# A residual added in PSUM by TensorE instead of on VectorE, in a bidirectional state-space block

## What is computed

```
xn  = layernorm(x)                                   # over the features
u_d = silu(conv4(win @ xn) + bias_d)                 # d = 0 forward, d = 1 on reversed time; 256 channels
delta, B, C = projections of u_d                     # softplus on delta
h[t] = exp(delta*A) * h[t-1] + delta*B*u             # 16 states for each channel, a scan over 512 tokens
y_d = sum over states (h * C) + D * u_d
attn = ((y_0 + reversed y_1) * silu(wz @ xn)) @ wout
ffn  = quantize(xn @ hadamard) @ ternary(w_ffn)      # 4 bits for each token
out  = x + attn + ffn                                # x is the residual
```

## Time and profile before

| | us |
|---|---|
| median of three runs | 885.19 (882.79 to 886.70) |
| the profiled execution | 887.24 |
| its span from first to last instruction | 885.2 |

### The profile page before, as it was taken

One profiled execution on the slowest core, in us unless ns is written; L12 is line 12 of the kernel. 1 busy time (PEld: TensorE's weight loads), 2 busy tenths in 40 slices (PEclk: granted clock), 3 DMA queues, 4 the chain that ended last, 5 costly groups with the idle time before them and its releaser, 6 DMA issues. The chain is left out here.

```text
span 885.2 us, 12125 instructions
## 1 busy us (share of the span) xinstructions
PE 757.5 (86%) x3953; PEld 390.4 (44%) x3953; DVE 798.4 (90%) x855; ACT 779.7 (88%) x1436; POOL 729.3 (82%) x355
## 2 busy tenths in 40 slices
PE   8867978799897988989799798979989897997885
PEld 6324445253543535344363445435353443634353
DVE  3849899998999999998999989999999989999996
ACT  2699997999979998999989999899989999898870
POOL 0176979798896988889697888979888896978994
PEclk9978999989999999999999999999999999999797
DMA  6435126070441608143180614506071430706100
GB/s 182 124 73 143 37 79 127 3 179 4 120 94 38 145 4 188 31 109 70 38 181 4 162 21 104 112 32 151 4 178 39 104 76 33 174 3 154 26 25 13
DMA packets 55119, 74.83 MB, mean 85 GB/s; under 512 B 6784, under 2 KB 23568, under 8 KB 55056
## 3 DMA queue, kind: packets, MB, share of 16 engines
q1 hardware_dynamic: 54624, 73.79, 35.7%
q10 hardware_dynamic: 432, 0.26, 0.1%
HBM read 62.49 MB, written 11.53 MB: 84 GB/s over the span
## 5 line engine op out<-in xcount | busy, mean ns | idle before, releaser
L752 POOL TENSOR_TENSOR hst<-hst,c_rep 128x1024 f32<-128x1024 f32 x255 | 598.6, 2372 | 103.0 <-DVE hst L627 90.6
L627 DVE TENSOR_TENSOR_SCAN hst<-da,b_ps 128x512 f32<-128x512 f32 x512 | 581.7, 1199 | 27.1 <-issue 21.0
L433 ACT ACTIVATE da<-rep,neg_a 128x511 f32<-128x511 f32 x504 | 331.5, 709 | 6.0 <-DVE hst L627 5.8
L964 PE MATMUL b_ps<-ident,dbx_t 128*128 128x128 f32 x1536 | 238.6, 296 | 97.0 <-DVE hst L627 72.5
L964 PEld LDWEIGHTS b_ps<-ident,dbx_t 128*128 128x128 f32 x1536 | 181.6, 150 | 225.1 <-DVE hst L627 130.4
L420 ACT ACTIVATE dbx_t<-du_t,b_t 128x256 f32<-128x256 f32 x576 | 248.1, 495 | 2.6 <-PE b_ps L964 1.9
L985 PE MATMUL y<-hst,sum_sel 128*32 128x512 f32 x1024 | 149.3, 658 | 4.3 <-POOL hst L752 4.3
L869 PE MATMUL pb<-xnt,conv_wt 128*128 128x512 f32 x240 | 110.7, 604 | 1.6 <-ACT du_t L403 0.9
L762 POOL TENSOR_TENSOR dbx_t<-du_t,b_t 128x1024 f32<-128x1024 f32 x48 | 91.7, 1910 | 7.6 <-ACT du_t L403 7.6
L943 PE MATMUL b_ps<-t_log,spread_sel 32*128 32x512 f32 x256 | 88.8, 666 | 1.7 <-DVE hst L627 1.0
L616 DVE TENSOR_TENSOR b_ps<-b_ps,b_rep 128x1024 f32<-128x1024 f32 x64 | 77.9, 1218 | 3.6 <-PE b_ps L943 2.3
(11 more groups left out here) (135 smaller groups left out, 602.8 us busy)
## 6 DMA issues: line engine op xcount, KB each, us to landing
rep<-d_scr SPq DMA_DIRECT2D x128, 256.0 KB, 9.1
c_rep<-bc_scr SPq DMA_DIRECT2D x64, 256.0 KB, 4.8
d_scr<-t_pos SPq DMA_DIRECT2D x16, 512.0 KB, 3.0
b_rep<-bc_scr SPq DMA_DIRECT2D x64, 64.0 KB, 2.4
x_ln<-x SPq DMA_DIRECT2D x8, 256.0 KB, 3.3
x_res<-x SPq DMA_DIRECT2D x8, 256.0 KB, 3.0
out<-x_res SPq DMA_DIRECT2D x8, 256.0 KB, 7.5
rep<-x SPq DMA_DIRECT2D x7, 256.0 KB, 4.4
```

The lines of the kernel that those rows point to most:

```text
L433: nc.scalar.activation(da[s % 2][:, j, 1:L], rep[d][h][:, j, 1:L], ACT.Exp, scale=neg_a[:, d, h, j, q:q + 1]).then_inc(decay_done, 1)
L627: nc.vector.tensor_tensor_scan(hst[s % RING][:, j, :], da[s % 2][:, j, :], b_ps[:, j, :], 0.0, ALU.mult, ALU.add).then_inc(scan_done, 1)
L752: nc.gpsimd.tensor_tensor(hst[s % RING][:, two, :], hst[s % RING][:, two, :], c_rep[d][:, q:q + 1, :].broadcast_to([P, 2, L]), ALU.mult).t ...
L964: ins = tr(b_ps[:, j, P * c:P * (c + 1)], dbx_t[(NX * d + q - 1) % 2][:, c, NJ * h + j, :, :].rearrange("p r e -> p (r e)"), ident[:, :])
```

## The change

DVE's addition goes away. PE adds the residual instead: ahead of the other products of a token block stands a product of the identity matrix with `x_res`, which opens the sum in the bank. The bank then holds the finished output, and ACT copies it into `x_res` (`keep_out`). PE now waits for `xres_loaded` before it projects. ACT's copy stands in slot 5 of the units with `d = 1` from the second batch on, and once behind the loop for the last batch.

```diff
+            def keep_out(b):
+                act.wait_ge(out_filled, b + 1)
+                nc.scalar.activation(x_res[:, :, :], pb[:, 1, :].rearrange("p (c o) -> p c o", c=NC), ACT.Copy).then_inc(out_ready, 1)
...
                     if s == 5:
                         if d == 0:
                             z_sigmoid(b)
+                        elif not first(b):
+                            keep_out(b - 1)
                         inputs_t(d, U, 3, 2)
...
             batches(act, body)
             keep_xqt(NB - 1)
+            keep_out(NB - 1)
...
-            def add_residual(b, at):
-                dve.wait_ge(out_filled, b + 1)
-                dve.wait_ge(xres_loaded, DMA * (b + 1))
-                nc.vector.tensor_tensor(x_res[:, :, :], at.rearrange("p (c o) -> p c o", c=NC), x_res[:, :, :], ALU.add).then_inc(out_ready, 1)
...
-                    if s == 5 and d == 1 and not first(b):
-                        add_residual(b - 1, pb[:, 1, :])
...
-            add_residual(NB - 1, pb[:, 1, :])
...
                 pe.wait_ge(free, count)
+                pe.wait_ge(xres_loaded, DMA * (b + 1))
                 for c in cs:
                     at = slice(P * c, P * (c + 1))
-                    mm(pb[:, 1, at], xqt[:, at], wq_t[:, :], start=True, stop=False)
+                    mm(pb[:, 1, at], ident[:, :], x_res[:, c, :], start=True, stop=False)
+                    mm(pb[:, 1, at], xqt[:, at], wq_t[:, :], start=False, stop=False)
...
+            pe.wait_ge(xres_loaded, DMA * NB)
             for c in range(NC):
                 at = slice(P * c, P * (c + 1))
-                mm(pb[:, 1, at], xqt[:, at], wq_t[:, :], start=c == 0, stop=False, skip_group_check=True)
+                mm(pb[:, 1, at], ident[:, :], x_res[:, c, :], start=c == 0, stop=False, skip_group_check=True)
+                mm(pb[:, 1, at], xqt[:, at], wq_t[:, :], start=False, stop=False, skip_group_check=True)
```

## The result

| | us |
|---|---|
| before, median of four runs | 884.53 (882.79 to 886.70) |
| after, median of four runs | 920.65 (916.50 to 922.03) |
| ratio | 1.040 (95%: 1.036 to 1.044) |
| span of the profiled execution, before and after | 885.2 and 918.3 |

What follows compares the result with a forecast made beforehand. DVE (90% busy) led, ACT (88%) close; ACT's in-order list decides. Late `keep_dut` 27.7, clock 3.6, last batch 2.8, end 0.8: 34.9 us on a median of 885.19, so 920 us; range 904 to 932.

Steps and rivals of the forecast that it cites:

- ACT's lead turns into a stall: Slot 5, units with d = 1: ACT stands still before its copy until the projection ends, 7 to 8.5 us, seven times.
- DVE waits for the decays: Before slot 5's second pair of scans DVE idles 4 to 4.6 us for ACT's decays; the pair ends 2.8 us late.
- `keep_dut` is late and nothing behind it absorbs that: In units with d = 1, `keep_dut` starts 4.76 or 4.49 us late and each of six batches lengthens by its delay.
- part of the delay is absorbed: Rival: the convolution chain has slack, so only DVE's 2.8 us stay in each batch; 906 us, chance 0.14.
- The size per batch: Batches b = 1 to 6: 27.7 us for late `keep_dut` plus 3.6 us for the clock, 5.2 us each.
- the chain through ACT's stall: From ACT's wait in slot 5 to `keep_dut`: 4.76 or 4.49 us late in each of six batches, 27.7 us in all.
- The end: Last batch: DVE's second pair 2.8 us late; behind the loop, four more products 0.88 less 0.10 for the copy, 0.8 us.
- The clock's term: PE's clock falls after its wait in slot 5, so ACT waits 0.6 us a batch for `du`, 3.6 us in all.
- The products as such: Four identity products a batch on PE, 0.22 us each, make `out_filled` 0.88 us later.
- The faster rival: The wait before `keep_dut`, up to 3.89 us, hides the copy and DVE's gain shows; 877 us, chance 0.03.
- the 8.7 us that I had allowed as its most: Most that taking the addition off DVE could gain: eight additions, 5.4 us, plus the waits before them, 3.3 us.

Runs made afterwards that it cites:

- f_filler: The changed kernel plus 15 thrown-away 128x128 products on PE while it waits in slot 5 for ACT's inputs of slot 6; 920.53 us, 1.041.
- d_copy: The changed kernel with the copy given back to DVE at its addition's place; PE still adds the residual, ACT has nothing new; 893.35 us, 1.010.
- dcopy_z: d_copy plus five PE products with a matrix of zeros in slot 2 of every unit; 887.97 us, 1.004 against the kernel before.
- p3_slot7: The changed kernel with ACT's copy moved from slot 5 to slot 7, directly ahead of `keep_dut`; 885.30 us, 1.003 against the kernel before.
- before_z: The kernel before plus five PE products with a matrix of zeros in slot 2 of every unit; 885.51 us, 1.000.

## Why the prediction was right

The time (920 against 920.65) and the sign were right, and the mechanism is the one that was forecast. By its steps:

- **ACT's lead turns into a stall: right.** Forecast 8.4 us for unit (1, 1), measured 8.39. The six inner batches show 8.39, 6.89, 8.39, 8.45, 6.89 and 8.39. The last batch showed 5.21, well below the 7 to 8.5 that I had given for all seven (6.89 is just below it); I had not looked up ACT's lead there.
- **DVE waits for the decays: right.** Forecast 4 to 4.6 us, measured 4.49 in unit (1, 1); 27.6 us over seven, so less in some.
- **`keep_dut` is late and nothing behind it absorbs that: right.** This was the step with the largest weight and no direct row. Its wait fell to 7.5 us in all (forecast: below 8), its starts are 109.2 us apart (forecast: 108 to 110). The rival "part of the delay is absorbed" (906 us) falls with this. The moves of the copy confirm it: 900, 894 and 885 us.
- **The size per batch: slightly low.** Forecast 31.3 us over six batches, 5.2 each; measured 5.50. Split by the table above, the chain through ACT's stall, with the low stretch behind it, was forecast at 4.6 + 0.6 a batch and is 4.4; low stretches elsewhere add 1.1, for which the forecast had nothing. The first batch came to 2.7 instead of 5.4; if the head start of 2.1 us is added, it is 4.9. The end was forecast at 3.6 and came to 2.9. The errors offset each other; that the median is met to 0.7 us is partly luck.
- **The clock's term: near in size, wrong in place.** I had 0.6 us a batch for the wait that ACT has for the transposes of `du` at the lower clock. The low stretch came, where forecast, and ACT waited 0.0 to 0.4 us for it; by `f_filler` it costs 0.1 to 0.2 us a batch. The wrong step is the assumption that this is the place where the clock matters, and that elsewhere it stays as it was. The 1.1 us come from the other low stretches; the section on the hardware below has two such places.
- **The end: right.** Twelve groups of products instead of eight; the sum of states and DVE's product behind them:

```profile
907.44 0.46 PE L1110 MATMUL pb<-x_res,ident 128*128 128x128 f32 x2 [3.13 <-DVE y_gated L640]
...
911.92 1.06 PE L986 MATMUL y<-hst,sum_sel 128*32 128x512 f32 x8
...
913.05 0.69 DVE L640 TENSOR_TENSOR y_gated<-y,gate 128x512 f32<-128x512 f32 x1 [5.87 <-PE y L986]
```

  The products took 4.48 us instead of 2.69, 1.8 more and twice the 0.88 that I had added, since the low clock now fell on them; but then the sum of states ran at full clock, 1.06 instead of 1.94. From the first product to DVE's multiplication it is 5.61 against 4.69, 0.92 more.
- **The products as such (0.88 us a batch on the way to `out_filled`): right for the changed kernel.** On their own `d_copy` came out 2 us above the forecast interval for it, but not by the products' work, which costs 0.2 us a batch in `dcopy_z`: I had treated the clock as fixed when PE's work is moved by a microsecond.
- **The faster rival.** It was to decide where ACT's lead is smaller than the wait before `keep_dut`. `p3_slot7` realizes just this, and the gain did not come even so: of the 8.7 us that I had allowed as its most nothing showed. In unit (1, 1) PE's chain from the projection to `du` ended last. That this chain, and not another, holds every batch at 102.7 us is not shown. The rule of the Trainium skill (Perfetto Trace Analysis, section "Identifying the Most-Contended Engine"), to relieve the engine with the highest occupancy first, would have led astray in both versions: DVE fell from 90% to 87% in the changed kernel, and it became 4% slower; with the copy in slot 7 nothing was gained.

Of the 36.1 us, the moves of the copy account for 35 as the price of its place. The 5.50 us a batch split into 3.0 for the wait alone, 1.4 for copy and products behind it, and 1.1 for low stretches over those that the kernel before has too. Open is what decides where a low stretch falls, and so whether another execution would split in the same way: each kernel has one trace.

## What to carry to other kernels

An instruction put on another engine takes its wait with it: compare, in the timelines, when the new engine reaches that place of its list and when its input is ready, and what stands behind it. An engine that runs ahead should take over work at the last place before it waits anyway; there the same copy cost 2 us instead of 36. And a gain on the busiest engine is worth nothing at a place where another engine's chain ends just as late; in this kernel the version whose copy hardly waits was level with the original. When a probe adds work to every repetition, look for the one in which the gap that it should fill is missing: here that was the last unit, and it hid much of what the probe had gained.

## What the hardware showed that I had not expected

The same wait of PE, at the same place, is sometimes followed by a stretch at 1.2 GHz and sometimes not. In the kernel before PE waits 2.0 us for POOL's inputs in slot 5 of each unit with d = 0 but the first and the last. Here are the 2 us stretches that follow this wait, in unit (2, 0) and in unit (3, 0) (the clock is the number before the DMA's two):

```profile
300.00:302.00 2.00, 2.00 (x12) 0.65 (x11) 2.00 (x3) 2.00 (x5) 2.00 (x1) 1.00 1.02 209
```

```profile
403.00:405.00 2.00, 2.00 (x12) 0.54 (x10) 2.00 (x3) 2.00 (x6) 2.00 (x2) 0.50 1.05 212
```

The batches that contain such a stretch at this place were 105.2 us long, two of five; the three without were 102.7 to 102.8. The convolution behind it began 1.6 us later after `keep_dut` (405.38 - 350.62 against 301.05 - 247.89), about the 1.7 us of work lost in it, and DVE and ACT wait for this convolution. In `before_z`, where it is the only low stretch of its batch, it makes the batch 1.6 us longer. The other 0.9 us of the 2.5 in the kernel before go together with a second stretch: in these two batches, and in no other, one falls on PE's work right ahead of the projection of the unit with d = 1. In unit (3, 1):

```profile
444.00:446.00 2.00, 2.00 (x11) 1.67 (x10) 2.00 (x3) 2.00 (x6) 2.00 (x2) 0.50 1.06 242
```

In the changed kernel with the products of zeros a batch with the first stretch took 108.7 us and one without 106.5, here from copy to copy,

```profile
520.00:522.00 2.00, 2.00 (x10) 0.41 (x10) 2.00 (x2) 2.00 (x5) 2.00 (x2) 0.60 0.93 189
...
628.00:630.00 2.00, 2.00 (x8) 0.87 (x5) 2.00 (x3) 2.00 (x5) 2.00 (x2) 1.00 1.05 211
```

the first row lying between the copies at 458.74 and 567.42, the second between those at 567.42 and 673.94. Low stretches elsewhere cost next to nothing: one of 3.4 us in slot 2 is part of the batches of 102.73 us, against 102.67 without any, and the one behind ACT's stall costs 0.1 to 0.2 us (`f_filler`). In `d_copy` two of five batches had the stretch in slot 5; the other three had one of 6.8 us in slot 2 instead, and all five the one ahead of the projection. The products of zeros took all of these away but one, and the batches went from 105.8 to 103.2 us. That the spread of the runs of one kernel comes from how many batches are hit fits the three groups of `before_z`; for the kernel before (882.79 to 886.70 us) it is a guess, since each kernel has one trace only.
